# An attention and mixture-of-experts block: waiting scatters, earlier rank products, and expert products for two blocks each

## What is computed

```python
# x [16, 256, 128], float32; 16 heads of 64
x = x + attention(layernorm(x))     # q, k, v, softmax(q k / 8), output projection
x = x + ffn(layernorm(x))

def ffn(x):                         # T = 4096 tokens
    probs = sigmoid(x @ router_w.T + expert_bias)          # 160 experts
    top_w, top_idx = top_k(probs, 8)
    top_w = 2.5 * top_w / (sum(top_w) + 1e-9)
    h = silu(x @ w_gate[e].T)                              # 64 wide, per chosen expert
    routed = sum over the 8 chosen e of top_w[e] * (h @ w_down[e].T)
    shared = silu(x @ w_gate_shared.T) @ w_down_shared.T
    return routed + shared
```

## Time and profile before

| | us |
|---|---|
| median of 3 runs | 1049.58 |
| lowest, highest | 1049.19, 1052.98 |
| the profiled execution | 1049.12 |
| its span | 1047.3 |

### The profile page before, as it was taken

How to read it: one execution, slowest core, us unless ns; L and a number is a source line. 1 busy time by engine, 2 the same in 40 slices (tenths; PEclk the granted TensorE clock), 3 DMA queues, 4 the chain that set the end, 5 groups by cost and what they waited for, 6 DMA issues and landing times.

```text
span 1047.3 us, 30540 instructions
## 1 busy us (share of the span) xinstructions
PE 860.7 (82%) x8800; PEld 664.1 (63%) x8800; DVE 741.7 (71%) x2514; ACT 770.5 (74%) x2408; POOL 704.8 (67%) x884
## 2 busy tenths in 40 slices
PE   6999999999999999999999997898787766664000
PEld 5777777777777777777777775676565544443000
DVE  5568888888878868888888888777476555554223
ACT  6888888888888878888888887779999755565000
POOL 3235676677677666776776776635777777777775
PEclk9999999999999999999999999899999877788555
DMA  8915654444443311221221224688888766665221
GB/s 239 381 47 227 250 209 158 169 167 185 171 172 146 110 68 63 87 91 63 82 96 60 78 101 165 212 293 264 275 270 262 226 192 197 185 203 164 58 59 52
DMA packets 75993, 169.99 MB, mean 162 GB/s; under 512 B 13856, under 2 KB 24416, under 8 KB 75936
## 3 DMA queue, kind: packets, MB, share of 16 engines
q1 hardware_dynamic: 57248, 133.63, 36.3%
q0 software_dynamic: 16384, 33.59, 11.2%
q10 hardware_dynamic: 2304, 2.10, 0.6%
HBM read 66.50 MB, written 102.76 MB: 162 GB/s over the span
## 4 chain that ended last, share of the span: by engine, by line
PE 44%; POOL 18%; issue 13%; DVE 12%; ACT 6%; DMA 3%; DVEq 1%; ACTq 1%; POOLq 0%; SPq 0%
POOL yg L990 15%; PE psS L454 10%; PE psO L532 8%; PE psT L482 7%; PE psY L445 6%; PE psA L494 4%; PE psVM L445 3%; ACT p_sb L758 3%; DVE negmax L1314 2%; DVE w_b L1355 2%; DMA block_y<-y_b 2%; ACT w_b L834 1%; PE psS L643 1%; POOL slot_x L963 1%; ACTq L272 1%
## 5 line engine op out<-in xcount | busy, mean ns | idle before, releaser
L990 POOL DMA_INDIRECT yg<-block_y,pos_u x256 | 249.7, 975 | 100.7 <-issue 74.7
L963 POOL DMA_INDIRECT slot_x<-xn_src,slot_u x240 | 244.7, 1020 | 95.7 <-issue 53.5
L758 ACT ACTIVATE p_sb<-psS,negmax 128x256 f32<-128x256 f32 x512 | 236.1, 474 | 99.1 <-DVE negmax L1314 98.7
L925 POOL TENSOR_SCALAR p_sb<-p_sb,rinv 128x256 f32<-128x256 f32 x256 | 142.6, 565 | 117.3 <-DVE rinv L1263 113.7
L1314 DVE TENSOR_REDUCE negmax<-psS 128x2 f32<-128x512 f32 x256 | 164.1, 682 | 28.0 <-PE psS L454 27.7
L454 PE MATMUL psS<-qk_sb 64*128 64x256 f32 x1024 | 145.6, 403 | 2.3 <-ACT p_sb L758 2.3
L321 ACT COPY pT_sb<-psT 128x512 f32<-128x512 f32 x256 | 140.9, 617 | 4.3 <-PE psT L482 4.3
L532 PE MATMUL psO<-pT_sb,v_sb 128*64 128x256 f32 x1024 | 138.8, 391 | 1.6 <-ACT pT_sb L321 1.1
L482 PE MATMUL psT<-ident,p_sb 128*128 128x128 f32 x1024 | 133.5, 274 | 2.3 <-POOL p_sb L925 2.3
L1355 DVE COPY w_b<-w_all 128x192 f32 x497 | 104.6, 276 | 41.8 <-issue 20.8
L643 PE MATMUL psS<-xbT,w_b 128*64 128x64 f32 x1664 | 76.9, 239 | 57.0 <-DVE w_b L1355 38.0
(11 more groups left out here) (181 smaller groups left out, 1879.5 us busy)
## 6 DMA issues: line engine op xcount, KB each, us to landing
block_y<-zero SPq DMA_DIRECT2D x26, 1024.0 KB
xb<-slot_x SPq DMA_DIRECT2D x104, 256.0 KB
block_y<-y_b SPq DMA_DIRECT2D x96, 256.0 KB
slot_x<-zero SPq DMA_DIRECT2D x15, 1024.0 KB
w_all<-in_wgd_dram SPq DMA_DIRECT2D x16, 960.0 KB, 4.8
slot_x<-zero SPq DMA_DIRECT2D x1, 11264.0 KB, 41.5
yg<-block_y,pos_u POOLq DMA_INDIRECT x256, 2.4
slot_x<-xn_src,slot_u POOLq DMA_INDIRECT x240
```

Of the source, the lines that this page charges most:

```text
L758: act.activation(p_sb[:, (g - 1) % 2, h, qt, :], psS[:, h, qt * SEQ:(qt + 1) * SEQ], ACT.Exp, bias=negmax[:, (g - 1) % 2, h, qt:qt + 1], s ...
L925: pool.tensor_scalar(pq, pq, rinv[:, (g - 2) % 2, k // 2, k % 2:k % 2 + 1], 1.0, ALU.mult, ALU.mult).then_inc(s["pn_ok"], 1)
L963: pool.indirect_dma_start(slot_x, bass.IndirectOffsetOnAxis(ap=slot_u[:, int(last), i, j:j + 1], axis=0), (xn2 if last else xn2_src)[:, i, ...
L990: pool.indirect_dma_start(yg[:, r, k, :], None, block_y, bass.IndirectOffsetOnAxis(ap=pos_u[:, n, k:k + 1], axis=0)).then_inc(gat_last if ...
```

## The change

- **Weights in `w_b`** are laid out for pairs of blocks: for a pair, the two gate pieces of 64 columns stand side by side, and the two down pieces of each 64 columns too. So one copy still reads one run of 192 floats, and writes three pieces of 64 that start 128 apart. This holds for all groups.
- **From group 40 on (`JOINT_FROM`)** a gate matmul takes the weights of two blocks and the rows of both (128 x 128 out, 4 of them), and a down matmul multiplies 64 hidden units' rows of two blocks with the down weights of both (128 x 256 out, 4 of them). Half of each product is of a block with the other's weights and isn't used: silu and output copies pick the right parts, 2 and 4 instructions instead of 1 and 2.
- **Who copies:** VectorE all eight up to group 39 (`ACT_LATE` 40), then six (`W_LATE` 6).
- **Scatters:** those of sequence 14 from its fifth on, and all 16 of the last, wait for one more turned group each.
- **Rank products** of the last sequence stand behind the downs of group 0, into `psA`; the second downs wait for the distances. VectorE's `new_blocks` and the slot steps each come one group earlier.
- ScalarE copies its weights of group 2 before `ffn_input` of the last sequence. From gather 48 on only every sixth waits for turned groups (`PACE_LATE`).

```diff
-W_EARLY, W_LATE = 5, 4
-ACT_EARLY, ACT_LATE = 7, 28
+W_EARLY, W_LATE = 5, 6
+ACT_EARLY, ACT_LATE = 7, 40
+JOINT_FROM = RING * COMBINE_FROM
-PACE, PACE_HEAD, PACE_FROM = 3, 27, 33
+PACE, PACE_LATE, PACE_APART, PACE_HEAD, PACE_FROM = 3, 6, 48, 27, 33
+EARLY_SCAT, SCAT_FROM = 4, 9
-LEAD, LATE_RANKS, LATE_TABLE = 4, 4, 33
+LEAD, LATE_RANKS, LATE_TABLE = 4, 2, 33
...
-        w_b = sb("w_b", [P, RING, GB, INTER + D])
+        w_b = sb("w_b", [P, RING, GB // 2, 1 + D // INTER, 2, INTER])
+        def weights_at(r, i):
+            c, h = pair_of(i)
+            return w_b[:, RING - 1 - r, c, :, h, :]
+        def weights_from(e):
+            return w_all[:, bass.ds(e, 1), :].rearrange("p o (k i) -> p (o k) i", i=INTER)
...
+                for i in JOINT if is_joint(n, share) else ():
+                    c, _ = pair_of(i)
+                    m = pe.matmul(psS[:, par, c * 2 * HB:(c + 1) * 2 * HB],
+                                  w_b[:, RING - 1 - r, c, 0].rearrange("p h i -> p (h i)"),
+                                  rows_of[:, par, i:i + 3:2], start=True, stop=True)
...
+                for i in (0, 2, 4, 6) if is_joint(n, share) else ():
+                    k, j = i // 2 % 2, i // 4
+                    half = slice(k * INTER, (k + 1) * INTER)
+                    m = pe.matmul(ps[k][:, 0, j * 2 * D:(j + 1) * 2 * D], hidden[half, par, j * 2 * HB:(j + 1) * 2 * HB],
+                                  w_b[half, RING - 1 - r, 2 * j:2 * j + 2, 1:, k, :], start=True, stop=True)
...
                     if early == 3:
                         pe.wait_ge(s["ot_ok"], NSTEP)
+                        pe.wait_ge(s["d_ok"], B)
+                    downs((r - 2) % RING, n - 2, share)
+                    if early == LATE_RANKS:
                         pe.wait_ge(s["x1_ok"], B)
-                    downs((r - 2) % RING, n - 2)
+                        pe.wait_ge(s["mask_ok"], B)
+                        ranks(psA[:, 0, :])
...
                     if early == 1:
+                        weights_of(2, 2)
                         ffn_input(B)
                         keep_input(B)
-                        weights_of(2, 2)
...
+                        if last:
+                            pool.wait_ge(s["xt2_ps"], SCAT_FROM + n)
+                        elif late and n >= EARLY_SCAT:
+                            pool.wait_ge(s["xt2_ps"], n - EARLY_SCAT + 1)
                         pool.indirect_dma_start(slot_x, bass.IndirectOffsetOnAxis(ap=slot_u[:, int(last), i, j:j + 1], axis=0),
...
-                    if i % PACE == 0:
+                    if i % (PACE if i < PACE_APART else PACE_LATE) == 0:
...
-                    m = dve.tensor_copy(w_b[:, RING - 1 - r, i, :], w_all[:, bass.ds(e, 1), :].rearrange("p o i -> p (o i)"))
+                    m = dve.tensor_copy(weights_at(r, i), weights_from(e))
...
             group(4)
-            distances(B + 1, psT[:, (LATE_RANKS - 1) % 2, :])
+            distances(B + 1, psA[:, 0, :])
+            new_blocks(B + 1)
             group(5)
-            new_blocks(B + 1)
-            group(6)
             slot_numbers(B + 1)
             best_slots(B + 1)
-            for n in range(7, RING * LEAD):
+            for n in range(6, RING * LEAD):
                 group(n)
```

More of the change, by code:

```diff
@@ L802, in silu @@
                 wait(act, s["y_ps"], n - 1)
[L803 to L804 removed]
+                for h in range(2) if is_joint(n, share) else ():
+                    half = slice(h * INTER, (h + 1) * INTER)
+                    m = act.activation(h_b[half, par], psS[half, par, :].rearrange("p (k h t) -> p k h t", h=2, t=HB)[:, :, h, :],
+                                       ACT.Silu)
+                if not is_joint(n, share):
+                    m = act.activation(h_b[:, par].rearrange("p k t -> p (k t)"), psS[:, par, 0:GB // 2 * HB], ACT.Silu)
+                m.then_inc(s["h_ok"], 1)
             def stored(r, n, back):
@@ L825, in outputs @@
                 y = y_at(r, is_wide(n) if isinstance(n, int) else wide)
-                for k in range(2):
+                for k, h in [(k, h) for k in range(2) for h in range(2)] if is_joint(n, share) else []:
+                    half = slice(h * HB, (h + 1) * HB)
+                    m = act.copy(y[half, k::2, :], ((psY, psVM), (psO, psA))[par][k][half, 0, :].rearrange(
+                        "p (a h d) -> p a h d", h=2, d=D)[:, :, h, :])
+                for k in () if is_joint(n, share) else range(2):
                     m = act.copy(y[:, k::2, :], ((psY, psVM), (psO, psA))[par][k][:, 0, 0:RW // 2 * D].rearrange("p (a d) -> p a d", d=D))
@@ L865, in _ @@
                 experts(it)
-            with act.Fori(LEAD, ACT_LATE // RING - 1) as it:
+            with act.Fori(LEAD, WIDE_TO // RING) as it:
                 experts(it, share=False, wide=True)
-            for it in range(ACT_LATE // RING - 1, COMBINE_FROM - 1):
+            for it in range(WIDE_TO // RING, COMBINE_FROM - 1):
                 experts(it)
```

33 lines of the change are left out of this document (16 added, 17 removed).

## The result

| | before | changed |
|---|---|---|
| median, us | 1049.38 (4 runs) | 1067.61 (4 runs, 1066.07 to 1070.08) |
| ratio | | 1.0169, 95% interval 1.0148 to 1.0190 |
| profiled execution, its span | 1049.12, 1047.3 | 1066.07, 1064.0 |

A forecast was written before the change was run, and what follows sets the result against it. GpSimd's unbroken gathers from 714 us were taken as the bound. Rank products -1.7, longer copies in groups 7 to 23 +3.0 and a gather stall +2.1 gave +3.4 on 1049.12: 1052.6 us, range 1046 to 1060.

The forecast's parts named there:

- part 5: VectorE copying all eight weights up to group 39: gather 24 waits for the 39th turned group, stall +2.1 us.
- the spread: Slow gathers beside VectorE's combines fall differently in a new schedule: 3 us either way.
- F: Instant when VectorE finishes group 23's eight weight copies, 8.1 us before the first gather; forecast to move by +1.3 us.
- What bounds: From 714 us GpSimd's gathers run without rest; only their first start, a stall or slower gathers can move the end.
- Copies: VectorE weight copies writing three pieces: spacing goes from 0.17 to 0.27 us, a group takes 2.2 us instead of 2.02.
- the upper bound: For a weight copy written in three pieces: 96 more steps, +100 ns per copy; the lower one was no change.
- Part 1 and 2: VectorE before the first gather: moved rank products, -1.7 us from mask to group 7; longer copies, +3.0 in groups 7 to 23.
- Part 3: Scatters waiting for turned groups: the last ends some 7 us before the first gather may start, cost 0.
- part 4: ScalarE's weight copies of group 2 ahead of the transposed input fill its 1.59 us of waiting, cost 0.
- Part 7: Sparser gather waits from gather 48: they release at most 1.5 us of waiting, which came earlier, so cost 0.
- part 6: Joint products from group 40: TensorE 2.8 us a group, ScalarE +0.2, covered by the gathers' 3.75 us pace, cost 0.
- The second rival: Joint products hold groups up at a low clock: period 4.5 us, stall 8.1 at gather 48, 1063 us; chance 0.10.

The follow-up runs named there:

- sets 2, 3 and 5: Three rounds of follow-up kernels, mostly the changed kernel with parts undone or reordered; the kernel before took 1051.25, 1048.82 and 1049.84 us in them.
- c4b: Changed kernel with four weight copies on each of VectorE and ScalarE in groups 28 to 39, nothing else undone: 1.0070 of the kernel before.
- a1b: Changed kernel with weight copies of groups below 38 writing one run of 192 again, pieces of 64 from there on: 1.0074 of the kernel before.
- a6b: Changed kernel with VectorE's combines ahead of the weight copies of each turn of four groups from group 40 on: 1.0096 of the kernel before.
- a4: Changed kernel with single products throughout, pieces of 64 and VectorE's eight and six copies kept: 1.0114 of the kernel before.
- a7b: Changed kernel with four weight copies each on VectorE and ScalarE from group 28 on, also past group 40: 1.0264 of the kernel before.
- c3: Changed kernel with one run of 192 below group 38 and four copies on each engine in groups 28 to 39: 1.0050 of before, 1053.8 us.
- c5b: Changed kernel with one run below group 38, four copies each in groups 28 to 39, combines ahead of copies: 1.0004 of before, 1049.49 us.

## Why the prediction was wrong

In the terms of the prediction: +3.4 us was forecast on the gathers, +16.8 came. Of the 13.4 between them, 3.9 are the stall of part 5 (6.0 for 2.1), 8.4 a wait that has no term, 1.8 slower gathers, for which the spread allowed 3, and the first gather gave 0.8 back. F is, as there, the end of the copies of group 23.

**Right, and measured:** *What bounds* held: only the gathers moved the end. *Copies:* 0.27 apart was forecast, 0.26 measured, so the choice of the upper bound was right. The reason was right in part only: not the 3 pieces lose the rate (3 pieces to 3 pieces took 0.20), but 3 on one side and one run on the other. *Part 1 and 2:* the first gather at 715.5 was forecast, 714.65 came; groups 7 to 23 took 706.4 - 670.6 = 35.8 for 37.4, the mask to group 7 11.6 for 10.9. Over the changed kernel and sets 2, 3 and 5 the first gather came at 713.1 to 716.1 with pieces (5 kernels) and at 709.5 to 713.6 with one run (6, without the one with two loads): the means are 714.2 and 711.4, so the layout costs 2.7 us there (4.0 forecast: 3.0 in groups 7 to 23 and 1.0 in the fifteen copies before them), and the ranks part gives 2.7 (2.7 forecast without the longer copies). Kernels that are alike up to the first gather lie up to 4 us apart, so neither number is sharp. *Part 3:* scatters that wait, 0, as forecast; no run tests part 4 by itself. *Part 7:* no wait past gather 48, as forecast.

**Wrong, first: part 5, the stall for turned groups.** The sum was right and read at the wrong gather. It put the copies of group 36 at F + 38.4; they ended at F + 38.8. But I asked only at gathers 24 and 30 and called 24 the worst. Gather 18 wants 27 + 18/2 = 36 turned groups, for which the copies of group 33 are enough: F + 10 x 2.2 + 9.8 = F + 31.8, and some 2.4 for table and three products, F + 34.2, when gather 18 is due at F + 30.7: a stall of 3.5, from my own rows. It was 4.55. The copies of group 33 ended at F + 31.2, but from there to the end of the transposes of group 35 it took 4.4 us for 2.4, with the granted clock at 0.50; the one step that can be compared took 3.16 for 1.80, so the low clock has some 1.4 of it. All 9.8 us of router steps lie ahead of group 33, and only the table behind it: the margin is smallest right behind them. With gather 24 it made 5.5, and with gather 16, which waits for row numbers behind the copies of group 32 and has no term either, 6.0 where 2.1 was forecast. What the runs show as the cause is the count of copies: with four each in groups 28 to 39 all 6.0 are gone (`c4b`), with the shorter copy alone 3.7 are left (`a1b`).

**Wrong, second: a wait that has no term.** The gathers also wait for their buffer, and the combine that frees it stands behind the copies of group 43 in VectorE's queue. The edit that I priced on the way to turned groups makes that combine 12 us later (764.4 for 752.3), past the start of gather 32, and gather 40 meets the same again: 8.44 us. In the kernel before, gather 32 at about 754.7 had 2 us to spare. I had named VectorE a follower and did not ask who waits for it there. `a6b` shows that the order alone removes these waits; fewer copies (`c4b`, 6.7 left) and single products (`a4`, 5.2 left) only shorten them.

**Wrong, third: part 6, joint products at cost 0.** I put TensorE at 2.8 us a group and ScalarE at +0.2, held this against the gathers' 3.75 and let it pass. ScalarE's term was mis-sized: 3.42 us a group for 2.28, so +1.1. The prediction took 0.26 for each of three more instructions, the spacing of three in the kernel before; the six now stand 0.37 to 0.39 apart. The rate is still covered, by 0.3 us a group, and no longer with four weight copies on ScalarE (3.94, `a7b`). The delay of the first such groups is not covered: without joint products the waits for combines are 3.2 us shorter (`a4`). The second rival had named joint products as the cause. It wanted a period over 3.3 us by a low clock and a stall at gather 48. The period came, but from ScalarE and at a clock of 1.00, and nothing waited at gather 48: the gathers were 12 us later than forecast by then.

How the 16.8 us divide, by undoing, in the profiles: four copies each in 28 to 39 alone takes off 11.3 (`c4b`), one run besides 0.8 more (`c3`), combines first 5.7 more (`c5b`). Of the 5.7 only the 4.8 of waits are the order's doing: the first gather, 3.0 earlier, lies before every combine, and slow gathers took 2.1 more. By the ratios the three steps are worth 1.0, 0.2 and 0.5%. The parts overlap: one run alone was worth 4.9 in the profile and 1.0% by the ratios (`a1b`), as long as VectorE was the late one.

**The slow gathers** stayed 7 to 11 us in all kernels but one (5, where gathers stood most), and moved single results by up to 4. (In the kernel before the prediction counted seven gathers of 1.3 to 2.0 us; the trace has eight.) In the changed kernel, too, they meet the first multiply of a combine:

```profile
804.10 1.22 DVE L1409 TENSOR_TENSOR yg<-yg,wE_res 128x1024 f32<-128x1024 f32 x1
804.13 2.00 POOL L1037 DMA_INDIRECT yg<-block_y,pos_u  x1 [0.30 <-issue]
```

The Trainium skill ("SBUF — State Buffer", the port pair that VectorE and GpSimd share) says that an instruction with two SBUF inputs blocks GpSimd's reads; these rows agree, but no run took the multiply away, so the cause is not shown.

## What to carry over

A stall term worked out for one waiter must be asked for every one with the same margin, above all right behind a bundle of extra steps, where the due times have run on and the supply has not. Before moving work to an engine that "only follows", list who waits for anything in its queue behind the new work, buffers that it frees included; here the place of the combines was worth some 6 us (8.4 of waits less 2.2 that came back), as much as all the waits at gathers 16 to 24. And an experiment that undoes a split should undo it only in the stretch in question, or it puts a new bound into the next.

## What the runs showed of the hardware

- A VectorE copy of 192 floats takes 0.17 us with one run on both sides and with 2 pieces of 96 or 6 of 32 written from one run, 0.20 with 3 pieces read and written, and 0.26 with one run on one side and 3 pieces on the other.
- A register load of six numbers (811 ns at the least, median 1167, in one stretch; 807 and 815 in another) was slower than one of eight (594, median 611, in the same stretch as the first) and of four (342, 351). Why six is worst, these runs don't tell.
- Two loads of four, 369 each, cost a group more than one load of eight: 2.32 us for 2.01.
- ScalarE needs 0.37 us each for silu and output copies that stand back to back with half the partitions (64x256), where three with all partitions (128x256) stood 0.26 apart.
- With transfers late (before: 1186 and 1192 us), combines first made about 2% against the changed kernel (one execution, with copies added at its end) and 2.7% between two kernels that also differ in layout; with transfers in time, 0.7% and 0.5%.
